# Feed-forward half of a two-layer gated block: PSUM banks split in two rings, taps and slots placed anew

## The reference, cut to what matters

```python
def act_quant(x):
    scale = 127.0 / jnp.clip(jnp.max(jnp.abs(x), axis=-1, keepdims=True), 1e-05)
    return jnp.clip(jnp.round(x * scale), -128, 127) / scale
...
h = bit_linear(x, w1)                       # 512 -> 2048, ternary weights, x quantised by token
h = depthwise_conv1d(h.transpose(0, 2, 1), conv_w, conv_b)   # 3 taps along the tokens
h = jax.nn.silu(h.transpose(0, 2, 1))
return bit_linear(h, w2)                    # 2048 -> 512, h quantised by its token's maximum
```

## Time and profile before

| what | value |
|---|---|
| median of 3 runs | 1982.39 us (1982.03, 1982.39, 1984.4) |
| span of the profiled execution, first to last instruction | 1983.3 us |
| its own time outside the profile | not given; the span stands for it |
| busy: DVE, PE, ACT, POOL | 1743.9, 1599.7, 1485.4, 616.9 us |
| mean granted TensorE clock | 0.973 |
| stage C begins near | 1161 us |
| feed-forward alone, from the end of the attention | some 1648 to 1983 us |

### The profile page before, as it was taken

How to read it: one execution, slowest core, us unless ns; L and a number is a source line. 1 busy time by engine, 2 the same in 40 slices (tenths; PEclk the granted TensorE clock), 3 DMA queues, 4 the chain that set the end, 5 groups by cost and what they waited for, 6 DMA issues and landing times.

```text
span 1983.3 us, 24380 instructions
## 1 busy us (share of the span) xinstructions
PE 1599.7 (81%) x9442; PEld 718.8 (36%) x9510; DVE 1743.9 (88%) x2619; ACT 1485.4 (75%) x1098; POOL 616.9 (31%) x480
## 2 busy tenths in 40 slices
PE   6858966698557966785599969999999976888887
PEld 3212211122112211231244426666666632334432
DVE  6899998999999987898598877999998669999997
ACT  4899999999999999999354845554554357767771
POOL 1000000000000000000062236666666446887881
PEclk9999999999999999999799989999999988999998
DMA  5000200020000010000387753333332110432312
GB/s 199 1 0 29 79 11 1 22 75 22 1 1 1 22 54 1 1 11 1 110 312 291 265 172 100 112 112 112 107 100 81 43 37 27 79 61 70 57 43 74
DMA packets 116710, 143.66 MB, mean 72 GB/s; under 512 B 25327, under 2 KB 74607, under 8 KB 116211
## 3 DMA queue, kind: packets, MB, share of 16 engines
q1 hardware_dynamic: 116594, 142.10, 22.9%
HBM read 87.55 MB, written 50.33 MB: 70 GB/s over the span
## 4 chain that ended last, share of the span: by engine, by line
ACT 43%; PE 30%; DVE 19%; issue 4%; POOL 3%; DMA 2%; SPq 0%; DVEq 0%; another core or an unknown queue 0%; POOLq 0%; ACTq 0%
ACT unit L514 39%; PE psum L1647 5%; PE psum L1681 5%; PE psum L1633 3%; DVE hmax_parts L1429 3%; DVE psum L1418 3%; PE psum L1016 3%; PE psum L1010 3%; DVE unit L423 2%; PE psum L1657 2%; PE psum L1674 2%; POOL hidden L1837 1%; PE psum L1666 1%; PE psum L547 1%; DVE hidden_q L1453 1%
## 5 line engine op out<-in xcount | busy, mean ns | idle before, releaser
L514 ACT ACTIVATE unit<-unit 128x4096 f32<-128x4096 f32 x244 | 857.6, 3620 | 0.5 <-DVE unit L423 0.3
L423 DVE TENSOR_SCALAR unit<-feat_proj,text_proj 128x1024 f32<-128x1024 f32 x976 | 667.5, 747 | 67.2 <-PE psum L639 65.2
L639 PE MATMUL psum<-unit,w_pad 128*32 128x512 f32 x3904 | 474.8, 605 | 234.1 <-ACT unit L514 234.1
L639 PEld LDWEIGHTS psum<-unit,w_pad 128*32 128x32 f32 x3904 | 102.5, 109 | 557.3 <-ACT unit L514 398.6
L680 POOL TENSOR_SCALAR red<-red 128x8 f32<-128x8 f32 x4 | 2.0, 510 | 531.5 <-DVE red L321 531.5
L1820 POOL TENSOR_TENSOR h<-h,arow 128x512 f32<-128x512 f32 x104 | 135.7, 1318 | 73.0 <-ACT h L1582 72.8
L1699 PE MATMUL psum<-xq_block,w_q 128*128 128x512 bf16 x489 | 122.8, 391 | 27.5 <-ACT hidden L1601 21.3
L680 POOL TENSOR_SCALAR rstd<-mv 128x8 f32<-128x8 f32 (+1 forms) x5 | 1.7, 336 | 411.7 <-DVE mv L216 411.7
L547 PE MATMUL psum<-xnT,W_sb 128*128 128x512 f32 x256 | 125.2, 617 | 2.1 <-ACT xnT L465 2.1
L1589 ACT ACTIVATE psum<-h,conv_b_sb,conv_w_sb 128x512 f32<-128x512 f32 x112 | 86.2, 779 | 53.6 <-POOL h L1820 46.7
L1734 PE MATMUL psum<-w_q,hidden_q 128*128 128x512 fp8e4 x448 | 104.1, 386 | 20.8 <-ACT hidden_q L1612 12.3
(11 more groups left out here) (255 smaller groups left out, 2790.0 us busy)
## 6 DMA issues: line engine op xcount, KB each, us to landing
h_scratch<-h SPq DMA_DIRECT2D x44, 512.0 KB, 4.4
hin<-h_scratch SPq DMA_DIRECT2D x32, 704.0 KB, 4.7
xin<-in_x SPq DMA_DIRECT2D x8, 1024.0 KB, 6.7
tern_in<-in_w1T SPq DMA_DIRECT2D x16, 512.0 KB, 4.2
tern_in<-in_w2T SPq DMA_DIRECT2D x16, 512.0 KB, 6.8
x<-in_x SPq DMA_DIRECT2D x16, 512.0 KB, 3.7
x_scratch<-x SPq DMA_DIRECT2D x32, 256.0 KB, 2.0
x3in<-x_scratch SPq DMA_DIRECT2D x31, 256.0 KB, 3.1
```

Source lines behind the costliest of these rows:

```text
L423: ins = ve.tensor_scalar(units[:, n % 3, k, :], FP[:, bi % 2, k, :], TP[:, k, n:n + 1], None, ALU.add)
L514: ac.activation(units[:, n % 3], units[:, n % 3], ACT.Tanh).then_inc(unit_tanh, 1)
L639: mm = te.matmul(psum[k * TG:(k + 1) * TG, 3 + 2 * grp + half, :], w_pad[:, k, TG - 1 - tt:2 * TG - 1 - tt], units[:, n % 3, k, half * BAN ...
```

## The change

- **Two rings of three banks.** W1 writes `raw_bank` (banks 0, 1, 2) and may write again once RAW or VMID has read it. TAP0, or PTAP, writes `tap_bank` (banks 3, 7, 5) and waits for the SILU three chunks before (`bank_free`).
- **Taps in slots of their own.** TAPS becomes TAP1 and TAP2, placed apart, each with its own semaphore.
- **Maxima.** The second HMAX writes bank 6 in PSUM, waiting for its turn there. HM2 becomes one `scalar_tensor_tensor` of `hm[0]` and bank 6 with the clamp 1e-5 in it. The factor 1/127 moves into SROW's scale and into a constant `w_mean[:, 2]`, made once by a new instruction and wait at the end of stage B. S3 keeps only the reciprocal; the scale for OUT is made on ACT (HS2).
- **Slots.** N2 goes from 344 to 306, OFF2 from 3950 to 4120, and all entries of the feed-forward are new; waits count by slot (`nth`). SP's loads follow the slots of AROWMM and W1. The last block's own code keeps its instructions.

```diff
+        ve.tensor_scalar(w_mean[:, 2:3], w_mean[:, 1:2], tg[:, 3:4], INV127, ALU.mult, ALU.mult).then_inc(mean_done, 1)
+        V.wait_ge(mean_done, 3)
         ve.tensor_scalar(w_mean[:, 1:2], w_mean[:, 1:2], tg[:, 3:4], None, ALU.mult).then_inc(b_done, 1)
...
-    N1, N2, OFF2 = 216, 344, 3950
-    LEN1, LEN2 = 1198, 1023
+    N1, N2, OFF2 = 216, 306, 4120
+    LEN1, LEN2 = 1198, 925
...
-    W1 = (98, 152, 189, 199, 208, 245, 275, 317, 327, 337, 350, 393, 403, 413, 423, 433)
-    VMID = (284, 443, 449)
-    GMID = (172, 222, 232, 242, 267, 292, 333, 344, 358, 369, 452, 463, 506)
-    RAW = (128, 162, 199, 210, 261, 285, 327, 337, 352, 362, 430, 457, 462)
-    TAP0 = (184, 234, 255, 291, 297, 314, 346, 367, 383, 450, 466, 477, 484, 518)
-    TAPS = (209, 289, 302, 314, 338, 358, 371, 383, 395, 467, 479, 498, 523, 535)
-    PTAP = (253, 371)
-    SILU = (240, 303, 308, 320, 332, 378, 389, 394, 399, 404, 410, 490, 495, 512, 537, 549)
+    W1 = (0, 24, 17, 82, 89, 126, 141, 134, 148, 184, 235, 177, 228, 255, 263, 270)
+    VMID = (107, 228, 284)
+    RAW = (73, 77, 98, 120, 140, 158, 153, 167, 193, 243, 236, 274, 298)
+    GMID = (102, 110, 119, 224, 185, 232, 241, 215, 206, 250, 258, 303, 346)
+    TAP0 = (162, 172, 248, 218, 253, 287, 268, 293, 336, 368, 374, 393, 408, 420)
+    TAP1 = (212, 191, 256, 238, 261, 294, 278, 300, 358, 375, 386, 402, 418, 429)
+    TAP2 = (223, 206, 267, 250, 272, 305, 289, 316, 380, 391, 408, 424, 435, 441)
+    PTAP = (155, 337)
+    SILU = (229, 213, 224, 278, 259, 282, 312, 303, 358, 363, 388, 399, 415, 450, 442, 455)
...
-    HROUND = (798, 854, 910)
-    AROWMM = (0,)
-    HMAX = (408, 579)
-    HM2 = (620,)
-    S3 = (695,)
-    HS = (724, 764, 818, 871)
-    W2 = (796, 848, 905, 971)
-    OUT = (836, 892, 958, 1015)
+    HROUND = (669, 752, 809)
+    AROWMM = (7,)
+    HM2 = (523,)
+    S3 = (550,)
+    HS2 = (662,)
+    EDGE = (345, 456)
+    HMAX = (322, 461)
+    HS = (575, 617, 680, 763)
+    W2 = (665, 709, 803, 889)
+    OUT = (703, 762, 857, 923)
...
-    RING, OUT_BANK = (0, 1, 2, 3, 7, 5), 4
+    W1_RING, TAP_RING, OUT_BANK = (0, 1, 2), (3, 7, 5), 4
...
+    def bank_free(engine, n):
+        if n < len(TAP_RING):
+            bank = READ_BY[TAP_RING[n]]
+            engine.wait_ge(bank_read[bank], ATT_TURNS[bank])
+        else:
+            engine.wait_ge(silu2_done, nth((n - len(TAP_RING)) // HC, (n - len(TAP_RING)) % HC, SILU, CHUNKS))
...
-            for f, c, n in of(q, TAPS, VE_TAPS):
-                acc = hidden_bank(HC * f + c)
-                V.wait_ge(tap0_done, n + 1)
+            for f, c, n in of(q, TAP1, VE_TAPS):
+                acc = tap_bank(HC * f + c)
+                V.wait_ge(tap0_done, nth(f, c, TAP0, VE_TAPS))
+                scaled_by(V, f, c)
                 ve.scalar_tensor_tensor(out=acc, in0=h1[:, c, 1:BANK + 1], scalar=cw_sb[:, c, 1:2], in1=acc,
-                                        op0=ALU.mult, op1=ALU.add).then_inc(tap_step, 1)
-                V.wait_ge(tap_step, 2 * n + 1)
+                                        op0=ALU.mult, op1=ALU.add).then_inc(tap1_done, 1)
+            for f, c, n in of(q, TAP2, VE_TAPS):
+                acc = tap_bank(HC * f + c)
+                V.wait_ge(tap1_done, nth(f, c, TAP1, VE_TAPS))
                 ve.scalar_tensor_tensor(out=acc, in0=h1[:, c, 2:BANK + 2], scalar=cw_sb[:, c, 2:3], in1=acc,
-                                        op0=ALU.mult, op1=ALU.add).then_inc(tap_step, 1)
+                                        op0=ALU.mult, op1=ALU.add).then_inc(tap2_done, 1)
...
-                ve.tensor_reduce(hm[:, k, :], H2[f % 2][:, pairs].rearrange("p g t r -> p t g r"), AX.XY, ALU.max,
-                                 apply_absolute_value=True).then_inc(hmax_step, 1)
+                if k == 1:
+                    V.wait_ge(bank_read[6], turn[6]["hmax", f] - 1)
+                ve.tensor_reduce(psum[:, 6, :] if k else hm[:, 0, :], H2[f % 2][:, pairs].rearrange("p g t r -> p t g r"),
+                                 AX.XY, ALU.max, apply_absolute_value=True).then_inc(hmax_step, 1)
...
-                ve.tensor_tensor(hm[:, 0, :], hm[:, 0, :], hm[:, 1, :], ALU.max).then_inc(hmax_step, 1)
+                ve.scalar_tensor_tensor(out=hm[:, 0, :], in0=hm[:, 0, :], scalar=1e-5, in1=psum[:, 6, :], op0=ALU.max,
+                                        op1=ALU.max).then_inc(bank_read[6], 1)
...
-                ve.tensor_scalar(hs[:, f % 2, 0, :], hs[:, f % 2, 0, :], 1e-5, INV127, ALU.max,
-                                 ALU.mult).then_inc(s_step, 1)
-                V.wait_ge(s_step, 3 * f + 1)
                 ve.reciprocal(hs[:, f % 2, 1, :], hs[:, f % 2, 0, :]).then_inc(s_step, 1)
-                ve.tensor_scalar(hs[:, f % 2, 2, :], hs[:, f % 2, 0, :], w_mean[:, 1:2], None,
-                                 ALU.mult).then_inc(s_step, 1)
...
+            for f, k, n in before_last(at2(q, HS2)):
+                A.wait_ge(bank_read[6], turn[6]["hmaxT", f])
+                ac.activation(hs[:, f % 2, 2, :], hs[:, f % 2, 0, :], ACT.Copy,
+                              scale=w_mean[:, 2:3]).then_inc(out_scaled, 1)
...
+                b = n - len(W1_RING)
+                if b < 0:
+                    bank = READ_BY[W1_RING[n]]
+                    T.wait_ge(bank_read[bank], ATT_TURNS[bank])
+                elif b % HC in GP_MID:
+                    T.wait_ge(raw_copied, nth(b // HC, b % HC, RAW, GP_MID))
+                else:
+                    T.wait_ge(mid_ve, nth(b // HC, b % HC, VMID, VE_MID))
```

More of the change, by code:

```diff
@@ L1190, in flamingo @@
     HALF = HC // 2
-    N1, N2, OFF2 = 216, 344, 3950
-    LEN1, LEN2 = 1198, 1023
+    TILES = tuple(range(TPK))
+    N1, N2, OFF2 = 216, 306, 4120
+    LEN1, LEN2 = 1198, 925
     SHIFT = (0, 156)
@@ L1291, in flamingo @@
     turn[6] = turns(first("pv", PV), first("wo", WO), second("arow", AROWMM),
-                    second("hmaxT", HMAXT), second("srow", SROWMM))
+                    ("hmax", HMAX[1:], N2, NF - 1, OFF2), second("hmaxT", HMAXT), second("srow", SROWMM))
     turn[7] = turns(first("turn2", TURN2))
@@ L1307, in upto, with nth, of_half, scaled_by @@
         return f * len(chunks) + sum(1 for d in chunks if d <= c)
+    def nth(f, c, slots, chunks):
+        at = slots[chunks.index(c)]
+        return f * len(chunks) + sum(1 for s in slots if s <= at)
+    def of_half(f, k, slots, chunks):
+        return max(nth(f, c, slots, chunks) for c in chunks if c // HALF == k)
+    def scaled_by(engine, f, c):
+        if c in GP_MID:
+            engine.wait_ge(mid_gp, nth(f, c, GMID, GP_MID))
+        else:
+            engine.wait_ge(mid_ve, nth(f, c, VMID, VE_MID))
+    def bank_free(engine, n):
[4 more added lines that the diff above has]
+            engine.wait_ge(silu2_done, nth((n - len(TAP_RING)) // HC, (n - len(TAP_RING)) % HC, SILU, CHUNKS))
     def before_last(at):
         return [(f, i, n) for f, i, n in at if f < NF - 1]
-    END_BANK, LAST_BANK = RING[0], RING[1:1 + TPK]
+    END_BANK, LAST_BANK = 0, (1, 2, 3, 7)
     def attention_over(engine):
@@ L1592, in feed_forward @@
                 if c in PE_TAPS:
-                    A.wait_ge(tap_mm, SEL_SUMS + upto(f, c, PE_TAPS))
+                    A.wait_ge(tap_mm, SEL_SUMS + nth(f, c, PTAP, PE_TAPS))
                 else:
-                    A.wait_ge(tap_step, 2 * upto(f, c, VE_TAPS))
+                    A.wait_ge(tap2_done, nth(f, c, TAP2, VE_TAPS))
                 A.wait_ge(sc_mm, NT)
@@ L1704, in feed_forward @@
                 T.wait_ge(edges_done, edged(f, c))
[L1705 to L1708 removed]
+                scaled_by(T, f, c)
+                bank_free(T, HC * f + c)
                 for k in range(3):
[L1710 removed]
+                    mm = te.matmul(tap_bank(HC * f + c), tapd[:, j, k, :], h1[:, c, k:k + BANK], start=(k == 0),
                                    stop=(k == 2))
@@ L1817, in feed_forward @@
             for f, c, n in of(q, GMID, GP_MID):
-                G.wait_ge(raw_copied, n + 1)
+                G.wait_ge(raw_copied, nth(f, c, RAW, GP_MID))
                 G.wait_ge(bank_read[6], turn[6]["arow", f])
@@ L1823, in feed_forward @@
                 cs = slice(k * HALF, (k + 1) * HALF)
-                G.wait_ge(tap_step, 2 * upto(f, (k + 1) * HALF - 1, VE_TAPS))
-                G.wait_ge(tap_mm, SEL_SUMS + upto(f, (k + 1) * HALF - 1, PE_TAPS))
+                G.wait_ge(tap2_done, of_half(f, k, TAP2, VE_TAPS))
+                G.wait_ge(tap_mm, SEL_SUMS + of_half(f, k, PTAP, PE_TAPS))
                 if f % BPS == BPS - 1:
```

110 lines of the change are left out of this document (52 added, 58 removed).

## The result

| | before | changed |
|---|---|---|
| median, us | 1983.17 (1982.03 to 1984.4, 4 runs) | 1945.64 (1944.79 to 1948.19, 4 runs) |
| ratio of the runs | | 0.9815, 95% interval 0.9801 to 0.9828 |
| span of the profiled execution, us | 1983.3 | 1942.8 |

What follows compares the result with a forecast made beforehand. VectorE's instruction costs were taken to set the period. Way in -0.6, block 1 -4.3, six periods -28.0 and stage B +0.2 gave -32.7 from 1983.3, less 0.9 for the median: 1949.7 us; eight in ten between 1941 and 1965.

Steps and rivals of the forecast that it cites:

- Taps, 1.5 us a block: On VectorE, first taps placed apart from their second taps cost 0.67 instead of 0.77 us; bounds 0 and 1.5.
- The second rival: On VectorE, taps gain nothing from standing apart, since a semaphore between chained operations costs nothing extra: 1961.7 us, chance 0.08.
- HM2, 0.98: VectorE's combining of the maxima, with one operand in PSUM, falls from 1.64 to 0.66 us; bounds 0 and 1.0.
- S3, 1.3: On VectorE only the reciprocal stays, 0.1 instead of 1.40 us; gain 1.3 a block, mostly a wait behind POOL.
- rounding, 1.06: On VectorE, one HROUND of three falls from 2.28 to 1.22 us, away from POOL's work; bounds 0 and 1.06.
- The period, 37.2: Feed-forward time per block: 41.86 less 4.84 us of VectorE gains gives 37.0, plus 0.2 for PE's idle time.
- Block 0's last tap 0.6 us earlier: Way in from the attention: block 0's last tap starts at 1651.0 instead of 1651.56; bounds 1649 and 1660.6.
- Block 1, -4.3: Block 1's period falls from 39.19 to 34.9 us, the middle between 39.19 and a floor of 30.9.
- The way out, 0: After the last tap, VectorE waits for POOL's last HS instead of a w2 product: no change, bounds -1 and +2.
- The hand-offs (1): PE's idle time stays because in-order queues meet at three banks: period 39.5, time 1963.5 us, chance 0.16.
- The late start (3): The feed-forward's later place is not made good; block 0 ends its taps at 1660.6: 1959.3 us, chance 0.06.
- The slower rival (4): Three tap banks run dry at each reduction, VectorE idles 3.7 us twice a block: 1992.9 us, chance 0.05.

Runs made afterwards that it cites:

- the run with the pairs: The changed kernel with each first tap moved into its second tap's slot, so both stand back to back again: 1960.02 us, 14.4 over the changed kernel.

## Why the prediction was right, point by point

- *VectorE sets the period, before and after.* Right. Idle time on it is 0.06 us a block after, and each part put back costs about its own VectorE time: +2.2, +0.8 and +1.0 us on the period. That PE comes next is not borne out: with VectorE's reductions halved, 1.7 us less on PE changed nothing.
- *Taps, 1.5 us a block.* Right in mechanism, 1.9 in size, above my upper bound of 1.5. I took 0.77 against 0.67; the means are 0.78 with its wait against 0.66, and the second taps are cheaper too (0.66 instead of 0.68). The second rival, the rule cited from the Trainium skill, is excluded by the run with the pairs.
- *HM2, 0.98; S3, 1.3; rounding, 1.06.* Measured 1.05, 1.28 and 1.0, and for the reasons given: with the old form in the new slots most of the first two came back, and so did a part of the third when a rounding was moved beside POOL. The reduction into PSUM kept its 4.33 us.
- *The period, 37.2.* Measured 36.3. This is the largest error of the sum, 6 x 0.9 = 5 us: 0.4 is the taps, 0.2 the penalty that I added for PE's hand-offs, which didn't come, 0.2 today's idle time, which I left in and which went, and 0.1 the VMID that the sixth block lacks. PE is 96% busy without a wait of VectorE's to show for it.
- *Block 0's last tap 0.6 us earlier.* -4.1, of which 1.0 lies ahead of all changed steps; the step's own part is -3.1. My sum gives 1624 + 27.2 = 1651.2, not 1651.0. X3 of the last tile came at 1620.5, better than the 1624 forecast, although PE's first W1 waited 3.17 us for its load where I had counted 1 to 2.
- *Block 1, -4.3.* Measured -4.0. The middle of 39.19 and 30.9, by which I went, is 35.05 and not 34.9; 35.2 was measured. It is a guess between two bounds that came out well, not a mechanism that was shown.
- *The way out, 0.* Measured +0.9. As forecast VectorE waits for POOL's last HS, 3.52 us; that it would then wait 1.85 us for a load of x3 I had missed.
- *The time.* By spans 32.7 us were forecast and 40.5 measured, 7.8 too little. The medians come within 4.1 us of the forecast. The other 3.7 are which executions were profiled, a long one before and a short one after; that part of the agreement is luck.
- *The rivals.* The hand-offs (1) didn't bind, but the half reductions show them 0.3 us away: a further cut on VectorE alone would have run into them. The late start (3) did not occur, but was near: 60 slots more cost 10 us, with the load of block 0's input as the last wait. The slower rival (4), dry banks, did not occur: VectorE waited 0.3 us for a TAP0 in six blocks.

## What to carry to other kernels

Where one in-order engine is busy over 98% of a steady period, price each of its instructions by the distance to the next start, not by its recorded length: the wait of a second tap for the first, and that of a two-input form or a scale beside POOL, are inside that distance, and the latter looks like work. Placing something independent between two dependent VectorE instructions (1.9 us a block), or moving one of two SBUF inputs to PSUM (1.0), gained here as much as taking the scales away (1.3). But the taps placed apart in the old order, with one ring, lost time: look at what such an edit does to the other queues. And where a start is moved, read in SP's order when its load will be issued.

## What the runs showed that I had not expected

- Taking half of the w2 matmuls off PE made the kernel 8.5 us slower: the granted clock of the stretch was 0.97 instead of 1.00, and only the blocks in which it fell, with W1 matmuls of 0.43 instead of 0.22 us, were longer.
- Four elements cost VectorE 1.28 us beside POOL, six times what they take when it is silent.
- Halving both reductions, 4.1 us a block on the busiest engine, gained 0.3.
